# Attention stage of a two-layer kernel: another order of the small jobs between the score blocks, and one VectorE list for both halves of a head pair

## The reference

```
qkv = X @ W_qkv                              # 16 heads of 64
scores = einsum('bqhd,bkhd->bhqk', q, k) / 8
weights = softmax(scores, axis=-1)
attn = einsum('bhqk,bkhd->bqhd', weights, v)
return attn.reshape(b, s, h * d) @ W_out
```

## Time and profile before

| | us |
|---|---|
| median of 3 runs (lowest to highest) | 1828.82 (1826.97 to 1830.44) |
| the profiled execution | 1841.47 |
| its span, first to last instruction | 1839.6 |
| PE busy | 1727.4 (94%) |
| DVE busy | 1547.9 (84%) |
| ACT busy | 1459.2 (79%) |
| POOL busy | 1444.4 (79%) |

### The profile page before, as it was taken

The page is one execution under the profiler, slowest core; times in us unless marked ns, Lnnn a source line. Parts: engine busy times, 40 slices in busy tenths (PEclk is TensorE's granted clock), DMA queues, the critical chain, the costliest instruction groups (busy, mean ns, idle before and its releaser), DMA issues. The chain is left out here.

```text
span 1839.6 us, 32373 instructions
## 1 busy us (share of the span) xinstructions
PE 1727.4 (94%) x9247; PEld 924.8 (50%) x9247; DVE 1547.9 (84%) x2180; ACT 1459.2 (79%) x1954; POOL 1444.4 (79%) x869
## 2 busy tenths in 40 slices
PE   5899999999999999999999999999999899975687
PEld 5444444444444444444444444444444677763456
DVE  7888888888888888888888888888888878888886
ACT  4488888888888888888888888888888777864553
POOL 5388888888888888888888888888888256654664
PEclk9899999999999999999999999999999999997899
DMA  7212121212212121212122121212122777331000
GB/s 258 79 36 80 36 80 46 80 46 69 78 52 86 34 80 36 80 46 80 46 69 82 51 83 34 80 36 80 46 80 62 241 218 218 115 99 48 0 18 29
DMA packets 125334, 143.31 MB, mean 78 GB/s; under 512 B 26737, under 2 KB 106673, under 8 KB 122098
## 3 DMA queue, kind: packets, MB, share of 16 engines
q1 hardware_dynamic: 120306, 132.61, 23.6%
q0 software_dynamic: 4992, 10.27, 1.7%
HBM read 87.20 MB, written 27.64 MB: 62 GB/s over the span
## 5 line engine op out<-in xcount | busy, mean ns | idle before, releaser
L1562 POOL TENSOR_TENSOR psum_k<-psum_k,probs 128x1024 f32<-128x1024 f32 x384 | 929.3, 2420 | 103.9 <-ACT probs L1499 83.8
L1499 ACT ACTIVATE probs<-ps_s 128x1024 f32<-128x1024 f32 x512 | 497.0, 1024 | 149.9 <-PE ps_s L1319 149.9
L1328 PE MATMUL ps_v<-probs,V 128*64 128x512 f32 x2056 | 497.8, 605 | 0.0
L1581 DVE TENSOR_REDUCE mxh<-ps_three 128x2 f32<-128x1024 f32 x264 | 318.5, 1207 | 98.3 <-PE ps_three L1286 98.2
L1483 ACT ACTIVATE ps_s<-peak 128x1024 f32<-128x1024 f32 x224 | 245.1, 1132 | 0.0
L1483 ACT ACTIVATE ps_s<-qkv_raw 128x1024 f32<-128x1024 f32 x224 | 245.0, 1131 | 0.0
L1622 DVE RECIPROCAL e_y_row<-e_y_row 128x128 f32<-128x128 f32 x256 | 241.0, 941 | 0.0
L1328 PEld LDWEIGHTS ps_v<-probs,V 128*64 128x64 f32 x2056 | 124.8, 136 | 228.6 <-issue 209.7
L1319 PE MATMUL ps_s<-e_ew 64*128 64x512 f32 x1536 | 199.0, 391 | 0.0
L1562 POOL TENSOR_TENSOR psum_k<-probs 128x1024 f32<-128x1024 f32 x64 | 152.8, 2388 | 47.2 <-ACT probs L1499 39.4
L854 POOL DMA_INDIRECT results<-e_y_row,e_y_at x92 | 102.6, 1115 | 82.0 <-ACT e_y_row L795 52.8
(11 more groups left out here) (320 smaller groups left out, 3184.4 us busy)
## 6 DMA issues: line engine op xcount, KB each, us to landing
e_ew<-w_split SPq DMA_DIRECT2D x23, 1024.0 KB
qkv_raw<-peaks SPq DMA_DIRECT2D x33, 512.0 KB, 3.9
V<-e_x_raw SPq DMA_DIRECT2D x33, 512.0 KB, 3.6
peak<-peaks SPq DMA_DIRECT2D x32, 512.0 KB, 4.3
xs_hi<-xh SPq DMA_DIRECT2D x16, 512.0 KB, 4.0
xs_lo<-xl SPq DMA_DIRECT2D x16, 512.0 KB, 5.0
rows<-in_blank_d SPq DMA_DIRECT2D x4, 1483.5 KB, 16.9
e_x_raw<-rows SPq DMA_DIRECT2D x23, 258.0 KB
```

Source lines behind the costliest of these rows:

```text
L1328: ins = nc.tensor.matmul(ps_v[rows, :], V[par][:, kt, rows], probs[:, t % RING, x, :], start=kt == 0, stop=kt == KT - 1)
L1499: nc.scalar.activation(probs[:, t % RING, :, :], ps_s[t % 2][:, :, :], ACT.Exp, scale=SCALE).then_inc(p_done, 1)
L1562: nc.gpsimd.tensor_tensor(acc, probs[:, (t - 1) % RING, :, :] if kt == 1 else acc, probs[:, t % RING, :, :], ALU.add).then_inc(add_done, 1)
L1581: nc.vector.tensor_reduce(mxh[:, kh, t, :], max_bank(unit, i)[:, :, :], AX.X, ALU.max).then_inc(m_done, 1)
```

## The change

The table `VISIT` is reordered. Before, its items by visit were K1 / Q0, den1 / out0 / V0 / Q1, den0 / out1 / V1 / K0: front, front, shared, shared, front, shared, shared, front. After, they are Q0, den1 / out0 / K1 / V0 / Q1, den0 / out1 / K0 / V1: front and shared visits alternate, and visits 4 to 7 are of the same kinds as 0 to 3. VectorE's seeds are those of steps 3 and 11 (before 3 and 13). ScalarE stages later weights in visit 4 instead of 5, GpSimd's L71 stands behind the add of step 9 instead of 11. VectorE's list is one function, called for each half.

```diff
-    VISIT = [("K1",), ("Q0", "den1"), ("out0",), ("V0",), ("Q1", "den0"), ("out1",), ("V1",), ("K0",)]
+    VISIT = [("Q0", "den1"), ("out0",), ("K1",), ("V0",), ("Q1", "den0"), ("out1",), ("K0",), ("V1",)]
-    BY_V = (3, 13)
+    BY_V = (3, 11)
-                    pe.wait_ge(xv_done, n * PER["v"] + AHEAD["v"])
+                    pe.wait_ge(xa_done, n * PER["a"] + AHEAD["a"])
-                    if p == 5:
+                    if p == VISITS // 2:
                         stage(n)
-                    if t != STEPS - 5:
+                    if t != STEPS - 7:
                         continue
-                step(0)
-                step(1)
-                low(n, "K1", nxt)
...
+                def half(hf, late, early, par):
+                    t = KT - KT * hf
+                    step(t)
+                    step(t + 1)
+                    low(n, early, nxt)
+                    seed(n, t + 3)
+                    row_max_upper(n, t + 2)
+                    row_max_lower(n, t + 2)
+                    row_max_shared(n, t + 3)
+                    inverse(n, hf, 0)
+                    inverse(n, hf, 1)
+                    add_out(n, f"out{1 - hf}")
+                    step(t + 4)
+                    step(t + 5)
+                    low(n, late, par)
+                    inverse(n, hf, 2)
+                    if hf:
+                        expert_part(n)
+                    row_max_upper(n, t + 6)
+                    row_max_lower(n, t + 6)
+                    row_max_shared(n, t + 7)
+                    inverse(n, hf, 3)
+                    normalise(n, hf)
+                half(1, "K1", "Q0", nxt)
+                half(0, "K0", "Q1", par)
```

More of the change, by code:

```diff
@@ L1385, in _ @@
                     p = t // 2
-                    b = (n + (2 if p == VISITS - 1 else 1)) // PAIRS % B
+                    b = (n + (2 if VISIT[p][0] == "K0" else 1)) // PAIRS % B
                     unit, i = maximum(t)
@@ L1502, in _ @@
                     if p not in SHARED:
-                        read(n, VISIT[p][0], par if p == VISITS - 1 else 1 - par)
+                        read(n, VISIT[p][0], par if VISIT[p][0] == "K0" else 1 - par)
                     for k in (t + 1, t + 2):
```

## The result

| | before | after |
|---|---|---|
| median | 1827.89 us (4 runs) | 1905.93 us (4 runs) |
| ratio to before | | 1.0426, 95% interval 1.0408 to 1.0444 |
| profiled execution | 1841.47 us | 1905.08 us |
| a pair | 42.08 us | 44.55 us |

The change makes the kernel 78 us slower, 4.3%. Forecast was 1919 with a range of 1838 to 1950. The median of before has one run more than the 1828.82 of the forecast. 32 pairs of 2.47 more make 79 us, so all of it lies in the attention loop: the last `add_out` starts at 1500.1 us, 77 later than before. The two profiled executions are only 64 us apart, since that of before took 416 us from there to its end and that of after 403.

What follows compares the result with a forecast made beforehand. TensorE, busy 99% of the attention loop, was taken to set the pace. The visits summed to 44.91 a pair against 42.08, 2.83 more, times 32 pairs 91 us: 1828.82 + 91 = 1919, range 1838 to 1950.

Steps and rivals of the forecast that it cites:

- `add_out` and two reciprocals ahead of the even maximum: VectorE's queue in visits 2 and 6 delays the even maximum, so the odd one starts at 2.47, not 1.83: 0.64 lost.
- `expert_part` caught by step 5's add: On VectorE, it takes 1.77 instead of 0.64 and delays visit 3's odd maximum from 1.72 to 2.77: 1.05 lost.
- `normalise(1)` caught by step 7's add: On VectorE, it takes 2.44 and delays visit 4's odd maximum from 1.83 to 3.11: 1.28 lost.
- one collision: Rival: expert_part is caught, but normalise starts ahead of step 7's add and visit 4 is on time; +50 us, 1878; chance 0.12.
- only the queue is longer: Rival: expert_part misses the adds and keeps 0.64, visits 3 and 4 are on time; 42.50 a pair, 1842; chance 0.12.
- `normalise(0)` costs nothing: Before the next pair's visit 0, it ends at 45.57; the even maximum comes at 45.49 where 45.46 was wanted: nothing.
- The sum: Eight visit lengths add to 44.91 a pair against 42.08: 2.83 more, times 32 pairs 91 us, 1919.
- The other edits at nothing: Moved VectorE and ScalarE seeds, L71, den1, V1's copy and SyncE's write make TensorE wait nowhere: no gain or loss.
- That alternation can give 0.86 a pair: With every visit at its best a pair takes 41.22 instead of 42.08: 0.86 less, 28 us over 32 pairs.
- the rule of the Trainium skill: VectorE with two SBUF inputs and a GpSimd instruction reading SBUF shut each other out; the second waits until the first is through.
- The tail: The VectorE instruction ends 0.55 or 0.28 after the GpSimd add it meets; without tails 27 us less, forecast 1892.

Runs made afterwards that it cites:

- e1: Changed kernel with expert_part moved from visit 2 to visit 1, between the even maximum's lower half and the odd maximum; 1830.36 us, 1.0019 of before.
- e3: Changed kernel with normalise(1) moved from the end of visit 3 to behind the even maximum of visit 4; 1873.15 us, 1.0261 of before.
- e5: Changed kernel with expert_part at its place but cut from 256 columns to 8; 1908.27 us, 1.0433 of before.
- e6: Changed kernel with each GpSimd add written as two instructions over half the columns, VectorE's list untouched; 1856.80 us, 1.0161 of before.
- e7: e4 with add_out ahead of the even maximum of visits 2 and 6 again; 1824.85 us, 0.9988 of before.
- e8: e7 with add_out cut from 512 columns to 8, most of the attention's output left out; 1802.53 us, 0.9872 of before.
- e4: Changed kernel with expert_part in visit 1, add_out and normalise(1) behind even maxima, and reciprocals in gaps ahead of odd maxima; 1828.94 us, 1.0013 of before.

## Why the prediction was right

The forecast's mechanism and its place were right; e1, e3, e5 and e6 show it. Step by step, against the visit lengths that it laid out:

| visit | predicted | measured | after e1 |
|---|---|---|---|
| 0 | 5.89 | 5.88 | 5.88 |
| 1 | 4.84 | 4.78 | 4.79 |
| 2 | 5.67 | 5.54 | 5.54 |
| 3 | 5.98 | 6.21 | 4.83 |
| 4 | 7.17 | 6.93 | 5.89 |
| 5 | 4.84 | 4.79 | 4.79 |
| 6 | 5.67 | 5.56 | 5.56 |
| 7 | 4.85 | 4.86 | 4.85 |
| pair | 44.91 | 44.55 | 42.13 |

- *`add_out` and two reciprocals ahead of the even maximum, 0.64 in visits 2 and 6.* Right; the size is 0.51 and 0.53. VectorE reached the maximum 1.09 into visit 2 (619.00 - 617.91), not 1.27: `add_out` took 0.63, and the two reciprocals and the small maximum stand a little closer than the rows of before had it. The cause is only half named: e7 and e8 show that it is `add_out` far more than the reciprocals. With one reciprocal fewer (e7) the visit came down by 0.1 to 0.2 only, with `add_out` all but gone as well (e8) to 5.08.
- *`expert_part` caught by step 5's add, 1.05 in visit 3.* Right in kind, 1.77 predicted and 1.92 measured, 1.36 lost and not 1.05 (the visit took 6.21 instead of 4.85), since visits 1 and 2 were shorter and it started earlier in the same add. Where such an instruction starts inside an add doesn't matter to its end.
- *`normalise(1)` caught by step 7's add, 1.28 in visit 4.* Right: 2.44 predicted, 2.22 measured, 1.04 lost and not 1.28. It started 0.71 into the add (629.12 - 628.41), so the room on the early side was there. That it followed from the first catch, the content of the rival "one collision" and "only the queue is longer", is what e1 shows: with `expert_part` out of the way it met step 6's add and cost nothing. e1's 1830 lies 12 us under the 1842 of that rival: 42.13 a pair, 42.50 predicted.
- *`normalise(0)` costs nothing.* Right, 1.14 to 1.16 long.
- *The sum.* 0.36 a pair too high, 12 of the 13 us: 0.24 in visits 2 and 6 and 0.24 in visit 4, less 0.23 in visit 3; the rest is 0.05 or 0.06 for each out item. That the errors of visits 3 and 4 cancel is luck; the mechanism doesn't need it, since either is under a quarter of what it stands for.
- *The other edits at nothing.* Nothing in the profile speaks against it: visits 0, 1, 5 and 7 are at their least. None of these edits was run by itself.
- *That alternation can give 0.86 a pair.* Too high, and the one step that failed, though nothing of the forecast hung on it. It took every front visit at 5.03, also those behind an out item. There `add_out` starts no earlier than 0.35 into the visit (e7), VectorE is wanted at 0.55, and the bank at 2.27. For this reason e4 ended 17 to 27 us above where I put it, and e7 10 to 17.

On the rule of the Trainium skill (SBUF — State Buffer, Who interferes with whom): the runs bear it out for both instructions, and e6 and e3 for the part that the trace of before could not show, that a shorter or absent GpSimd instruction shortens the wait or takes it away. The tail behind the wait goes with the number of columns: 0.55 for 512, 0.28 for 256, 0.03 for 8. In before, after and e1 to e7, every `normalise` that started inside an add or half-add ended 0.54 to 0.56 after it, and every `expert_part` of 256 columns 0.28 or 0.29. The tail didn't decide the forecast: without it this would have been 1892, 14 us below the 1906 measured, where 1919 is 13 above.

What stays open: the differences of a few us between the sums of visits and the medians (e7's pair of 41.97 is 0.1 shorter than that of before, 3.5 us, where 2.2 were measured).

## What to carry to other kernels

Look for VectorE instructions with two operands in SBUF while GpSimd works on SBUF, and give each the time to the end of the GpSimd instruction that it meets and a tail behind that (here 0.55 for 512 columns, 0.28 for 256), not its own; then place it where GpSimd idles or where nothing urgent stands behind it. Moving one that takes 0.4 us by itself was worth 75 us here, and a lateness ahead of it moved the next one from a harmless add to a costly one. When one order of jobs is judged by its least times, add what reads a job's result to the visit behind it: a consumer that fits into no gap takes back what the order gives.

## What the runs showed of the hardware

- A subtraction over 8 columns with two SBUF operands took 1.66 us, because GpSimd was in a 2.39 us add; over 256 columns 0.42 with no add running (e1) and 1.92 in that add; a product over 512 columns 0.68 with GpSimd idle (e3) and up to 2.55 (e5). Such a wait stands in the profile as busy time of the VectorE instruction.
- GpSimd pays too: an add that started while `normalise` still ran took 2.7 us instead of 2.4, 64 of 64 times in e1 (2.73 in the add at 852.74).
- Cutting an add costs GpSimd time: half an add takes 1.29 us, the whole one 2.39 (e6).
- With VectorE idle, `add_out` started 0.28 us after the profile's end of the matmuls that it waits for (837.63 + 1.03 to 838.94, e7); ends of matmuls are modelled, and the cause is not shown.
